# A convolution of q in split products of 256 columns, inside a kernel of linear attention and an edge layer

## What is computed

```python
qkv = concat([h @ wq.T, h @ wk.T, h @ wv.T])
dw = conv(qkv, dw_kernel, 5x5, groups=3 * 512)
pw = conv(dw, pw_kernel, 1x1, groups=3 * 64)
f = concat([qkv, pw]).reshape(B, -1, 3 * 8, N)
query, key_, value = relu(f[:, :, :8]), relu(f[:, :, 8:16]), f[:, :, 16:]
scores = einsum('bhdn,bhen->bhde', [value, 1], key_)
out = einsum('bhde,bhen->bhdn', scores, query)
out = out[:, :, :-1] / (out[:, :, -1:] + EPS)
y = batch_norm(conv(out, proj_kernel, 1x1)) + x
```

## Time and profile before

| | |
|---|---|
| median of 3 runs | 4757.51 us (4748.52 to 4766.44) |
| the profiled execution's own time | 4761.0 us |
| its span | 4759.2 us |
| granted TensorE clock, mean | 0.971 |
| convolution of one head on TensorE | 5.30 us |
| heads in all | 256 |

### The profile page before, as it was taken

One profiled execution on the slowest core, in us unless ns is written; L12 is line 12 of the kernel. 1 busy time (PEld: TensorE's weight loads), 2 busy tenths in 40 slices (PEclk: granted clock), 3 DMA queues, 4 the chain that ended last, 5 costly groups with the idle time before them and its releaser, 6 DMA issues. The chain is left out here.

```text
span 4759.2 us, 70417 instructions
## 1 busy us (share of the span) xinstructions
PE 4475.4 (94%) x24296; PEld 3665.0 (77%) x24296; DVE 2811.9 (59%) x4023; ACT 2208.0 (46%) x3983; POOL 1239.6 (26%) x1030
## 2 busy tenths in 40 slices
PE   8999999999999999999999999589999999999968
PEld 7988988888888889888888888466666676666626
DVE  3354454454444444543544444279889978978996
ACT  3343333343333433433333334046576666666666
POOL 2442433433424424324334244000030020003003
PEclk9999999999999999999999999799999999999989
DMA  6685676676766766856767667767557746746613
GB/s 192 223 286 198 232 270 211 230 256 223 255 221 236 272 201 231 286 200 225 259 223 254 226 229 246 259 221 243 174 181 224 244 142 221 247 161 201 201 56 126
DMA packets 486662, 1045.54 MB, mean 220 GB/s; under 512 B 40624, under 2 KB 94512, under 8 KB 484016
## 3 DMA queue, kind: packets, MB, share of 16 engines
q1 hardware_dynamic: 486320, 1040.99, 65.1%
HBM read 665.02 MB, written 375.82 MB: 219 GB/s over the span
## 5 line engine op out<-in xcount | busy, mean ns | idle before, releaser
L807 POOL TENSOR_TENSOR toeplitz<-taps 128x512 f32<-128x512 f32 x768 | 895.7, 1193 | 932.3 <-PE bank L483 864.2
L483 PEld LDWEIGHTS bank<-toeplitz,columns 128*128 128x128 f32 x8192 | 964.3, 193 | 15.3
L483 PE MATMUL bank<-toeplitz,columns 128*128 128x128 f32 x8192 | 963.7, 276 | 0.0
L391 PE MATMUL bank<-x_hi,w_hi 128*128 128x512 f32 x1536 | 612.0, 398 | 19.8 <-DVE x_lo L655 19.8
L393 PE MATMUL bank<-x_lo,w_hi 128*128 128x512 f32 x1536 | 601.0, 391 | 0.0
L392 PE MATMUL bank<-x_hi,w_lo 128*128 128x512 f32 x1536 | 599.1, 390 | 0.0
L1530 POOL TENSOR_TENSOR centred<-centred,x_out 128x512 f32<-128x512 f32 x128 | 174.3, 1384 | 1606.8 <-ACT centred L1313 1605.1
L742 DVE TENSOR_SCALAR ckey_t<-bank 128x256 f32<-128x256 f32 x256 | 108.5, 424 | 807.5 <-PE bank L483 807.5
L473 PE MATMUL bank<-loaded,toeplitz 128*128 128x256 f32 x2048 | 510.9, 394 | 57.7 <-DMA loaded<-tiles_dram 42.1
L1163 PE MATMUL bank<-edge,w_branch 128*128 128x512 f32 x1024 | 483.2, 621 | 78.6 <-ACT edge L1261 78.6
L1149 PE MATMUL bank<-att_hi,w_proj_hi 128*128 128x512 f32 x1024 | 437.5, 427 | 62.3 <-DMA att_lo<-att_dram 51.2
(11 more groups left out here) (142 smaller groups left out, 7036.7 us busy)
## 6 DMA issues: line engine op xcount, KB each, us to landing
x_sb<-in_x_tiled SPq DMA_DIRECT2D x128, 1024.0 KB, 6.3
loaded<-tiles_dram SPq DMA_DIRECT2D x256, 433.5 KB, 5.9
tiles_dram<-tiles SPq DMA_DIRECT2D x112, 867.0 KB, 7.6
inverse<-inverse_dram SPq DMA_DIRECT2D x256, 256.0 KB, 7.7
att_dram<-out_hi SPq DMA_DIRECT2D x256, 256.0 KB, 4.1
att_dram<-out_lo SPq DMA_DIRECT2D x256, 256.0 KB, 5.1
att_hi<-att_dram SPq DMA_DIRECT2D x64, 1024.0 KB, 7.6
att_lo<-att_dram SPq DMA_DIRECT2D x64, 1024.0 KB, 10.5
```

The source lines that it names most:

```text
L391: nc.tensor.matmul(banks[t][:, :], wh, xh, start=(k == 0), stop=False)
L483: last = nc.tensor.matmul(bank[:, v * M:(v + 1) * M], columns[:, h % 2, t - T_K, v + b, a * HT:(a + TO) * HT], w[:, t, d, :], start=(d == ...
L807: last = nc.gpsimd.tensor_tensor(toeplitz[:, h % 2, t, :].rearrange("p (d o r) -> p d o r", o=HD, r=PL), tap, point, ALU.mult)
```

## The change

The convolution of q goes from four fp32 products a head to twelve fp32r ones of the same 256 columns, three for each shift. Both operands are split: the tile into `q_hi` and `q_lo`, the matrix into `tq_hi` and `tq_lo`. ScalarE makes the high parts as rounded copies, VectorE the low ones by subtraction. `q_lo` and `tq_lo` lie in the places of `loaded` and `toeplitz`; `q_hi` and `tq_hi` are new and single. They are made one head ahead: in pass h for head h+1. On ScalarE they come behind `q_stage` of h and ahead of `round_out`; on VectorE they are first in the pass, ahead of `divide`. Head 0's matrix is split at chunk 1 of `plain` and its tile at the end of `plain`, between `mask_scores` and `invert`. GpSimd builds head 0's matrices at chunk 0 instead of 3, and head 1's at 3 instead of 5. TensorE's q products wait for both splits.

```diff
@@ TensorE, conv_head
-                    x_q = loaded[:, h % LR, T_Q, :].rearrange("p (a c) -> p a c", c=TG)
-                    pe.wait_ge(tiles_loaded[h % LR], 16 * (SH // LR) * it + 16 * (h // LR) + 16)
-                    pe.wait_ge(toeplitz_ready, SH * it + h + 1)
+                    wide = tq_hi[:, :].rearrange("p (d m) -> p d m", m=M)
+                    x_hi_q = q_hi[:, :].rearrange("p (a c) -> p a c", c=TG)
+                    x_lo_q = q_lo[:, h % LR, T_Q, :].rearrange("p (a c) -> p a c", c=TG)
+                    pe.wait_ge(q_split, SH * it + h + 1)
+                    pe.wait_ge(tq_split, SH * it + h + 1)
                     if h >= 2:
                         pe.wait_ge(cevac[T_Q], SH * it + h - 1)
                     for d, (a, b) in enumerate(SHIFTS):
-                        last = nc.tensor.matmul(q_bank[0:M, 0:TT], w[:, T_Q, d, :], x_q[:, a:a + TO, b:b + TO],
-                                                start=(d == 0), stop=(d == len(SHIFTS) - 1))
+                        high, low = x_hi_q[:, a:a + TO, b:b + TO], x_lo_q[:, a:a + TO, b:b + TO]
+                        narrow = tq_lo[:, h % 2, T_Q, d * M:(d + 1) * M]
+                        nc.tensor.matmul(q_bank[0:M, 0:TT], wide[:, d, :], high, start=(d == 0), stop=False)
+                        nc.tensor.matmul(q_bank[0:M, 0:TT], narrow, high, start=False, stop=False)
+                        last = nc.tensor.matmul(q_bank[0:M, 0:TT], wide[:, d, :], low, start=False, stop=(d == len(SHIFTS) - 1))
                     last.then_inc(cready[T_Q], 1)
 
+                    pe.wait_ge(toeplitz_ready, SH * it + h + 1)
                     pe.wait_ge(columns_ready, SH * it + h + 1)
@@ ScalarE, plain: at chunk 1, between round_x and key
+                        if j == 1:
+                            round_taps(it, 0)
@@ ScalarE
+                def round_q(it, h):
+                    act.wait_ge(tiles_loaded[h % LR], 16 * (SH // LR) * it + 16 * (h // LR) + 16)
+                    copy(q_hi[:, :], loaded[:, h % LR, T_Q, :]).then_inc(q_rounded, 1)
+
+                def round_taps(it, h):
+                    act.wait_ge(tq_built, SH * it + h + 1)
+                    copy(tq_hi[:, :], toeplitz[:, h % 2, T_Q, :]).then_inc(tq_rounded, 1)
@@ ScalarE, conv
+                    round_q(it, 0)
                     gather(it, 0)
                     for h in range(SH):
                         if h + 1 < SH:
...
                         nc.scalar.activation(q_stage[:, h % 2, :], CONV_BANKS[T_Q][h % 2][0:M, 0:TT], ACT.Relu).then_inc(cevac[T_Q], 1)
+                        if h + 1 < SH:
+                            round_q(it, h + 1)
+                            round_taps(it, h + 1)
                         if division(it, h, started):
                             round_out(*division(it, h, started))
@@ VectorE
+                def split_q(it, h):
+                    dve.wait_ge(q_rounded, SH * it + h + 1)
+                    nc.vector.tensor_tensor(q_lo[:, h % LR, T_Q, :], loaded[:, h % LR, T_Q, :], q_hi[:, :].bitcast(F32), ALU.subtract).then_inc(q_split, 1)
+
+                def split_taps(it, h):
+                    dve.wait_ge(tq_rounded, SH * it + h + 1)
+                    nc.vector.tensor_tensor(tq_lo[:, h % 2, T_Q, :], toeplitz[:, h % 2, T_Q, :], tq_hi[:, :].bitcast(F32), ALU.subtract).then_inc(tq_split, 1)
@@ VectorE, plain
                         compress(it, j)
+                        if j == 1:
+                            split_taps(it, 0)
...
                     mask_scores(it, 0)
+                    split_q(it, 0)
                     invert(it, 0)
@@ VectorE, conv
                     for h in range(SH):
+                        if h + 1 < SH:
+                            split_q(it, h + 1)
+                            split_taps(it, h + 1)
                         if division(it, h, started):
                             divide(*division(it, h, started))
@@ GpSimd, build: q's matrix is reported by itself
+                        if t == T_Q:
+                            last.then_inc(tq_built, 1)
@@ GpSimd, plain
-                        if j in (3, 5):
-                            build(it, j // 2 - 1)
+                        if j in (0, 3):
+                            build(it, j // 3)
```

More of the change, by code:

```diff
@@ L83, in attention @@
         cvalue_t = sb("cvalue_t", [P, HV * PL, P + 1])
-        loaded = sb("loaded", [P, LR, 3, TN])
+        with nc.sbuf_tensor("loaded", [P, LR, 3, TN], F32) as loaded:
+            pass
+        q_lo = ctx.enter_context(nc.sbuf_tensor("q_lo", [P, LR, 3, TN], F32R))
         columns = sb("columns", [P, 2, 2, HV + 1, TG * HT])
-        toeplitz = sb("toeplitz", [P, 2, 3, len(SHIFTS) * M])
+        with nc.sbuf_tensor("toeplitz", [P, 2, 3, len(SHIFTS) * M], F32) as toeplitz:
+            pass
+        tq_lo = ctx.enter_context(nc.sbuf_tensor("tq_lo", [P, 2, 3, len(SHIFTS) * M], F32R))
+        tq_hi = ctx.enter_context(nc.sbuf_tensor("tq_hi", [P, len(SHIFTS) * M], F32R))
+        q_hi = ctx.enter_context(nc.sbuf_tensor("q_hi", [P, TN], F32R))
         q_stage = sb("q_stage", [M, 2, TT])
@@ L156, in attention @@
         toeplitz_ready = sem("toeplitz_ready")
+        tq_built = sem("toeplitz_q_built")
+        tq_rounded = sem("toeplitz_q_rounded")
+        tq_split = sem("toeplitz_q_split")
+        q_rounded = sem("q_tiles_rounded")
+        q_split = sem("q_tiles_split")
         cready = [sem(f"conv_{n}_ready") for n in "qk"]
```

## The result

The changed kernel takes 4901.66 us (median of 5 runs, 4897.78 to 4903.5), the kernel before 4757.51 (5 runs as well). The ratio is 1.030, with a 95% interval of 1.028 to 1.031: slower by 144 us. The sign was forecast; the size was not: 5110 us is a loss of 350 us, where 144 were measured.

What follows compares the result with a forecast made beforehand. TensorE bounds the kernel before; after the change a ScalarE-VectorE loop bounds chained heads. +361 for 172 heads, -25 for 84, +14 for starts and build make +350 on 4761.0, so 5110 us was predicted, range 4890 to 5230.

Steps and rivals of the forecast that it cites:

- The sign and the mechanism of the loop: Convolution heads: slower, chance 0.93, as ScalarE and VectorE wait for each other once a head and TensorE follows.
- 7.4 forecast: One loop round: 3.16 us of ScalarE, 4.10 of contended VectorE, 0.06 of hand-overs and 0.1 of split_q.
- rival 3: Convolution: VectorE's stretch stays under 2.1 us, the loop does not bind, every head gains 0.3; 4698 us, chance 0.06.
- rival 4: TensorE's q group: narrow fp32r products bring nothing at 0.19 us each, q is 2.3 us; 5186 us, chance 0.02.
- the other 11 at T, in 15 iterations; in the first iteration 7. That is 172 heads: Chained convolution heads: all but each run's first take a full round T of 7.4 us, +361 us.
- 5.3 or less, or one above 9: Loop lengths T in us at which GpSimd's products and VectorE's stretch would keep apart; otherwise 4.10 us contended.
- Rival 2: TensorE in chained heads: gaps of 2.4 us lower the clock, each head loses 1.8 us; 5421 us, chance 0.10.
- Rival 1: Convolution loop: it binds, but GpSimd covers only half of VectorE's stretch, T about 6.2; 4905 us, chance 0.14.
- not 1.44: TensorE's q group: twelve narrow products at 0.12 us each make 1.44 us, and a head 5.0.
- The 25 us that the other 84 heads were to gain: Convolution heads outside the chained 172: each 0.3 us faster at TensorE's pace, -25 us in all.
- Head 0's start and the moved build: Iteration starts and projection: 0.5 us for head 0's wait, 0.4 for the build, 16 times, +14 us.
- The 7.7 of the prediction: Round length T in us if VectorE and GpSimd exclude each other for whole instructions; some 52 us more in all.

Runs made afterwards that it cites:

- e1: The changed kernel with VectorE's divide moved ahead of the two subtractions of the pass, so the loop is open; 4759.27 us.
- e2: The changed kernel, but from head 2 on GpSimd builds only q's matrix, with a 16-column product replacing those for k and v; 4739.72 us.
- e5: The changed kernel with one more wait: GpSimd starts head h+2's matrices only after the division of pass h has been multiplied; 4809.42 us.
- e3: The changed kernel with one more fp32 product of 512 columns on TensorE behind heads 4 to 12, filling part of the gap; 4997.52 us.
- e6: The changed kernel with mixed_weights moved from pass 3 to 12, its write and the next weights load to passes 13 and 15; 4853.84 us.
- e9: e1 with mixed_weights in pass 12, the taps' load issued at the end of the even pass before, and the weight split in pass 14; 4727.11 us.
- e10: e9 with the first two heads' matrices built at chunks 3 and 5 and head 0's matrix split at chunk 5; 4722.02 us.

## Why the prediction was wrong

**The sign and the mechanism of the loop were right.** That `divide` behind `split_taps` closes a loop between ScalarE and VectorE, that it costs the reads shared with GpSimd, and that TensorE then follows it, was seen in the rows of before. e1, e2 and e5 take away the loop, the contention and their overlap, each alone, and each takes back most of the loss. The size of a round was right too: 7.4 forecast, 7.25 measured (rival 3, a stretch of 1.70 throughout, and rival 4 fall).

**The step that failed** is "the other 11 at T, in 15 iterations; in the first iteration 7. That is 172 heads". Above all the count of rounds was wrong, not their price. The 172 intervals have a mean of 6.10 us where 5.33 stood before: +133 us instead of +361. With the clock up, in e3, their mean is 6.71, which splits the difference:

- From 7.4 to 7.25, or 26 us, is the price of a round.
- From 7.25 to 6.71, or 93 us: the run does not begin behind the first head. In iterations 1 to 15 of e3 as of the changed kernel, heads 3, 4 and 5 start 5.39, 5.07 and 5.69 us after the one before, which is 84 of the 93. The prediction asked at which T GpSimd and VectorE keep apart and answered "5.3 or less, or one above 9". It then took that as excluded, though a loop of 4.9 alone lies under TensorE's head. In these early heads TensorE bounds at 5.07, the roundings come early in the head, and GpSimd is through before the division. It lasts until `mixed_weights`, or, without it, for some three heads more (e6). Pass 2 of the changed kernel:

```profile
312.30 3.76 POOL L852 TENSOR_TENSOR toeplitz<-taps 128x512 f32<-128x512 f32 x3 [3.73 <-PE bank L500]
...
315.06 1.54 DVE L750 TENSOR_TENSOR tq_lo<-toeplitz,tq_hi 128x512 fp32r<-128x512 f32 x1
316.53 1.08 DVE L724 TENSOR_TENSOR out_sb<-relu_c,inverse 128x256 f32<-128x256 f32 x2
```

- From 6.71 to 6.10, or 105 us: the clock, as far as e3 parts it from TensorE's longer head there. Rival 2 had the right observation, that the gaps would bring a low clock, and the wrong sign. It asked whether the loop hides the slow head, which it does, and not what else waits for a head's end. GpSimd does, and one late start ends the contention for three or four heads. The low clock saved time.

Rival 1, "late heads push the build behind it", at 4905 us and a chance of 0.14, names this second part and comes within 4 us. That nearness is in part luck: its derivation, contention over half of every stretch, is not what happened. Most rounds are nearly whole or nearly free.

**Other terms.** A q group is 1.56 us (322.74 to 324.30), not 1.44; a head is 5.07, not 5.0. The 25 us that the other 84 heads were to gain did not come: the 68 of their intervals that lie inside the convolutions add up to 409 us before and after. The loop costs in one of them too: from head 1 to head 2 it is 6.81 us where 6.16 stood, and 5.61 in e1, with the loop open. From head 14 to head 15 it is 5.51 where 5.30 stood, and 5.10 in e9, with the weight split moved. Head 0's start and the moved build were forecast at 14 us in all. Outside the convolutions the span grew by 4; the moved build is there as forecast, and e10 gives it 5 us, where the prediction had 0.4 x 16 = 6:

```profile
402.19 3.60 POOL L852 TENSOR_TENSOR toeplitz<-taps 128x512 f32<-128x512 f32 x2
...
402.27 2.60 DVE L686 TENSOR_TENSOR x_lo<-x_sb,x_hi 128x1536 fp32r<-128x1536 f32 x1 [5.15 <-ACT x_hi L546]
```

**How the two engines share.** The prediction set two stretched records against the Trainium skill's rule ("SBUF — State Buffer", section "Who interferes with whom") that two such instructions exclude each other for a whole instruction. The trace of the changed kernel agrees with the rule. 91 times `q_lo` starts with 0.32 to 1.03 us of a GpSimd product still to run. However much that is, `q_lo` ends 0.31 to 0.32 us behind the product, so its record is anything from 0.64 to 1.35 us long instead of 0.46; the row of 1.36 in e5 is such a case, beside a product that ends at 330.48. The other way round it is the same: of the two products in the lines above, the first takes 1.06 us and the second, which starts while `x_lo` runs, 2.59. So the engines take turns, and the wait lies inside the record of the one that waits. In the contended stretch of 4.08 us each of VectorE's three instructions waits for one product. The 7.7 of the prediction added the two engines' times whole, though some 0.14 us of them overlap at each change of turn (0.46 alone, 0.32 behind a product), so its distance to the measured 7.25 says nothing against the rule.

**What stays open.** Why the narrow products are worth so little in the open kernel was not followed further. That VectorE and GpSimd set its passes 5 to 11 fits their 5.3 us, but no run took GpSimd's reads out of the open kernel. After which of the gaps the clock falls was not tried either; only that none brought a low clock once they were filled.

## What to carry to other kernels

Before a split or a copy goes ahead of another engine's work in a queue, follow the waits until they either end or come back to where they began: here ScalarE's `round_out` came back to `round_taps`, and moving one call by one place was worth 142 us by the medians. Where such a loop's length depends on its phase to a third engine, do not stop at one steady state: ask in which phase the kernel starts, how long it stays there, and what in the steady state itself could end it. A filler, a slower product or a lower clock can move such a phase, so a small change of any engine may give or take more than its own time.

## What the runs showed of the hardware

- fp32r products with 256 columns follow each other every 0.13 us (12 in 1.56), against 0.227 with 512 and 0.216 for an fp32 record with 256.
- A 512-column subtraction and the two multiplications on VectorE took 1.70 us alone and 4.08 beside GpSimd's products of two SBUF operands, and these 3.96 instead of 3.08. They take turns by whole instructions: a `q_lo` of 289 columns that started during a product ended 0.31 to 0.32 us behind it, in all 91 cases with 0.32 to 1.03 us of the product left.
- After gaps of 1.95 us, one to three of them 7.25 us apart, the granted clock was 0.50 for 3.4 us (21 times from head 2 to head 15 of the changed kernel); with 1.0 us of products in each gap, and gaps of 1.07 us, it stayed at 1.00 from head 2 on in every convolution.
